# A gated slot attention block with a linear layer: the first tiles of the last phase begin a step sooner, between the products of the last step

## The chip, the core and the metric

The kernel runs on one core of one Trainium2 chip. The metric is the device time of one launch in microseconds (us); lower is better. Nothing else runs on the chip.

## The reference

Four sequences of 512 rows with 512 columns go through an attention block with 16 heads of width 128 and 64 memory slots per head, then a residual sum and layer norm, then a linear layer (called FFN here) with its own residual sum and layer norm. What follows is the core of it (float32):

```python
q, k = rope(hs @ Wq.T), rope(hs @ Wk.T)              # 16 heads of 128
v, g = hs @ Wv.T, hs @ Wg.T
s = clip(hs @ Ws1.T @ Ws2.T + bs2, -32, 32)          # 64 slots per head
es, enz = exp(s), exp(-cumlogsumexp(s, axis=time))
A  = mask(q k^T) * scale
ok = enz * (A @ es);  qv = softmax(ok)
W2 = mask((qv * enz) @ es^T);  o = W2 @ v
o_g = o * rsqrt(mean(o*o) + EPS) * g_norm_weight * (g * sigmoid(g))
x = layernorm(hs + o_g @ Wo.T)
out = layernorm(x + x @ (weight * scale_weight[:, None]).T + bias)
```

## The kernel before, in words

**Steps.** The 2048 rows are 16 chunks of 128, the 16 heads are 4 groups of 4. One step does one chunk for one group, so there are 64 steps (STEPS), four chunks of a sequence in a row (c = 0 to 3), unrolled by `all_steps_in_line`. `left` is the number of chunks still to come in the sequence where this is the last sequence of the last group: it is 1 in step 63 and 0 in step 64; in most steps it is 4. A step projects the next chunk (q, k, v, gate) and does the attention of this one. Matrix products in float32 are split into a high and a low part (names `_hi`, `_lo`): three products of 128x512 for each of four column blocks, which makes 12 instructions (`product`, line 874). The gated and normalised output `o_gated` of a step is transposed into `oT`, split into `oT_hi` (ScalarE) and `oT_lo` (VectorE), multiplied by Wo in the next step and added by VectorE to a partial sum `part`, which SyncE stores to a scratch in DRAM and loads again for the next group.

**Last phase.** 16 tiles of 128 rows go through norm, linear layer and norm. A function `tick(t, s)` on each engine does tick t: VectorE takes the statistics of tile t (`first_stats`, `first_mean_var`, `first_neg_mean`, `first_var_eps`), adds the linear layer's product of tile t-4 to its residual, takes that one's statistics, and between them makes the low part of the transposed rows of tile t-2. GpSimd makes x1 + bias of tile t-2 and two powers (1/sqrt of var + eps) for tile t and tile t-4. ScalarE makes the high part of the transposed rows of tile t-1, the normalised rows x1 of tile t, and the output rows z of tile t-4, and issues the store of these. TensorE makes the linear layer's 12 products of tile t-2 and 4 transposes of x1 of tile t. Ticks 0 to 3 stand inside step 64 (`if not left`) and behind it, tick 4 to 7 are written out (`last_phase`), then a loop runs.

**Order.** Every engine executes its own instructions in the order in which they are written, and waits on semaphores that the others raise. So where a `tick` is written in `step` sets what it waits behind and what waits behind it. In step 64 before: TensorE does the okT products (line 983, 988), the transposes of step 63's o_gated (L888), tick 0 (transposes of x1 row tile 0, L961), okT's transposes, prob's transposes (L888, 128x128 x2), step 63's Wo product (bank_a), the w2 and states products (L1051, L1055), tick 1, tick 2 (product of tile 0 and transposes of tile 2), the o products (L1076); then, behind the step, tick 3, the last transposes of o_gated, the last Wo product (`last_out`) and tick 4. VectorE does tick 0 before `ok_scaled`, tick 1 before `part`, tick 2 before `mask_w2`, tick 3 after it. GpSimd does `o_norm` of the step before first (a power L429 and a product L431, which normalise o_gated), then the ticks. ScalarE does tick 0 first, ticks 1 and 2 before `o_sq`, tick 3 behind the step, then `oT_hi`.

**Names in the trace.** A buffer that is used again keeps its first name: the raw rows of the last phase and x1 are `w_raw`, the transposed rows' parts are `w_hi` and `w_lo` (`bank_c`, `bank_e`, `bank_a`, `bank_wo` are their banks), the linear layer's products are written into `bank_qv`, `bank_kg`, `bank_t` and `bank_wo`, and z into `gate`, `masked` and `rope_a`. `x1 + bias` goes to `q_rot`, `k_rot`, `qT`. The two banks `bank_s` and `bank_o` are the halves of `bank_wo`.

## Time and profile before

| | us |
|---|---|
| median of three runs | 1488.28 (1487.54, 1488.28, 1490.73) |
| the profiled execution | 1487.25 |
| its span in the trace | 1485.4 |
| TensorE busy (page, part 1) | 1455.7 (98% of the span) |
| VectorE, ScalarE, GpSimd busy | 912.0, 526.9, 506.5 |
| mean granted TensorE clock | 0.998 |

The profile has one page with the busy time of each engine and, behind it, a trace of each instruction. In the timeline a line is the start (us from the span's start), the duration, the engine (PE is TensorE, DVE VectorE, ACT ScalarE, POOL GpSimd, SPq and ACTq DMA issues by SyncE and ScalarE), the line of the kernel, what is written and read, how many instructions are merged, and in brackets the idle time before it with the engine that ended it. The duration of a matmul includes its way through the array, so that two in a row overlap; the distance between two starts is what one costs. Steps 63 and 64 end at about 1409 and 1427 us; the last store is issued at the end of the span.

### The profile page before, as it was taken

The numbers are of one execution on the slowest core, as the hardware profiler recorded it, in microseconds if no ns is written. First come the engines' busy times: TensorE is split into PE (matmuls) and PEld (weight loads), VectorE is DVE, ScalarE is ACT, GpSimd is POOL, SyncE is SP. The second block draws the span as 40 slices with busy tenths as digits, with TensorE's granted clock in tenths as the row PEclk, the third lists the DMA queues.
The fourth block names the chain that finished last, engine by engine and source line by source line (L and its number), as shares of the span: only waits on it lengthen the run. The fifth ranks groups of instructions, "written<-read, shape, count | busy, mean of one in ns | idle before, by whom it ended". The sixth has DMA issues, their size and how long they took to land.

```text
span 1485.4 us, 22855 instructions
## 1 busy us (share of the span) xinstructions
PE 1455.7 (98%) x9152; PEld 1193.2 (80%) x9152; DVE 912.0 (61%) x1651; ACT 526.9 (35%) x1013; POOL 506.5 (34%) x440
## 2 busy tenths in 40 slices
PE   6999999999999999999999999999999999999988
PEld 4888888888888888888888888888888888888866
DVE  6656556566665656556765655656765565656677
ACT  5323323234322323333332333323433332324256
POOL 2333233233242233224423322422432242333245
PEclk9999999999999999999999999999999999999999
DMA  5101102122111202112320211112221111202123
GB/s 205 65 22 62 53 22 72 38 84 99 65 58 43 72 22 72 43 36 79 135 72 22 72 43 36 58 43 93 86 99 44 36 58 43 71 22 78 65 89 124
DMA packets 39558, 96.60 MB, mean 65 GB/s; under 512 B 4384, under 2 KB 4384, under 8 KB 35744
## 3 DMA queue, kind: packets, MB, share of 16 engines
q1 hardware_dynamic: 37152, 90.98, 18.3%
q10 hardware_dynamic: 2304, 4.20, 0.8%
q8 instruction: 72, 1.18, 0.3%
q14 instruction: 30, 0.25, 0.1%
HBM read 74.19 MB, written 20.97 MB: 64 GB/s over the span
## 4 chain that ended last, share of the span: by engine, by line
PE 89%; POOL 5%; DVE 2%; issue 2%; ACT 1%; DMA 0%; SPq 0%; POOLq 0%; DVEq 0%; ACTq 0%
PE bank_kg L874 25%; PE bank_qv L874 22%; PE bank_a L874 12%; PE bank_t L888 7%; PE bank_wo L1076 4%; POOL o_gated L431 3%; PE bank_a L909 3%; PE bank_e L901 3%; PE bank_wo L1051 3%; PE bank_wo L983 2%; PE bank_c L1081 2%; PE bank_wo L1055 1%; POOL rms L429 1%; PE bank_c L1086 1%; PE bank_wo L916 1%
## 5 line engine op out<-in xcount | busy, mean ns | idle before, releaser
L429 POOL TENSOR_TENSOR rms<-var,minus_half 128x4 f32<-128x4 f32 x64 | 65.2, 1018 | 594.2 <-DVE var L846 594.2
L874 PE MATMUL bank_qv<-w_hi,hs_hi 128*128 128x512 f32 x512 | 209.6, 409 | 7.2 <-DVE w_lo L627 6.8
L874 PE MATMUL bank_kg<-w_hi,hs_hi 128*128 128x512 f32 x512 | 207.6, 406 | 3.3 <-DVE w_lo L627 3.3
L874 PE MATMUL bank_qv<-w_hi,hs_lo 128*128 128x512 f32 x512 | 204.1, 399 | 0.0
L874 PE MATMUL bank_qv<-w_lo,hs_hi 128*128 128x512 f32 x512 | 203.4, 397 | 0.0
L874 PE MATMUL bank_kg<-w_hi,hs_lo 128*128 128x512 f32 x512 | 202.7, 396 | 0.0
L874 PE MATMUL bank_kg<-w_lo,hs_hi 128*128 128x512 f32 x512 | 201.9, 394 | 0.0
L874 PE MATMUL bank_a<-wo_hi,oT 128*128 128x512 f32 x504 | 171.8, 402 | 0.0
L400 POOL TENSOR_TENSOR k_rot<-rope_a,rope_b 128x512 f32<-128x512 f32 x64 | 82.6, 1290 | 223.6 <-DVE rope_b L656 223.6
L697 DVE RECIPROCAL enzT<-cumsT 128x256 f32<-128x256 f32 x64 | 112.2, 1753 | 63.9 <-ACT cumsT L514 51.7
L465 ACT ACTIVATE oT<-bank_t 128x512 fp32r<-128x512 f32 x64 | 38.3, 598 | 262.6 <-PE bank_t L888 262.6
L396 POOL TENSOR_TENSOR q_rot<-rope_a,rope_b 128x512 f32<-128x512 f32 x64 | 82.6, 1290 | 115.0 <-DVE rope_b L656 115.0
L874 PEld LDWEIGHTS bank_qv<-w_hi,hs_hi 128*128 128x128 f32 x512 | 97.5, 190 | 26.1 <-issue 7.5
L874 PEld LDWEIGHTS bank_qv<-w_hi,hs_lo 128*128 128x128 f32 x512 | 96.9, 189 | 23.4
L874 PEld LDWEIGHTS bank_kg<-w_hi,hs_lo 128*128 128x128 f32 x512 | 96.1, 188 | 23.1
L874 PEld LDWEIGHTS bank_kg<-w_hi,hs_hi 128*128 128x128 f32 x512 | 96.3, 188 | 21.3 <-DVE w_lo L627 2.5
L874 PEld LDWEIGHTS bank_qv<-w_lo,hs_hi 128*128 128x128 f32 x512 | 97.3, 190 | 17.4
L874 PEld LDWEIGHTS bank_kg<-w_lo,hs_hi 128*128 128x128 f32 x512 | 96.4, 188 | 17.6
L874 PEld LDWEIGHTS bank_a<-wo_hi,oT 128*128 128x128 f32 x504 | 94.8, 188 | 18.1
L798 DVE TENSOR_REDUCE ok_max<-bank_wo 128x4 f32<-128x256 f32 x64 | 27.2, 424 | 132.4 <-PE bank_wo L1015 132.4
L431 POOL TENSOR_TENSOR o_gated<-o_gated,rms 128x512 f32<-128x512 f32 x64 | 98.2, 1534 | 5.0
L827 DVE TENSOR_TENSOR part<-bank_a,part 128x512 f32<-128x512 f32 x63 | 43.4, 690 | 91.6 <-PE bank_a L874 91.6
(163 smaller groups left out, 2921.3 us busy)
## 6 DMA issues: line engine op xcount, KB each, us to landing
w_raw<-w_groups SPq DMA_DIRECT2D x28, 1024.0 KB, 4.8
hs_raw<-hs_cols SPq DMA_DIRECT2D x64, 256.0 KB, 2.8
x_scratch<-part SPq DMA_DIRECT2D x64, 256.0 KB, 2.0
part<-x_scratch SPq DMA_DIRECT2D x48, 256.0 KB, 2.7
w_raw<-w_groups SPq DMA_DIRECT2D x16, 256.0 KB, 6.1
part<-hs_rows SPq DMA_DIRECT2D x16, 256.0 KB, 2.7
w_raw<-x_scratch SPq DMA_DIRECT2D x16, 256.0 KB, 2.7
out<-gate ACTq DMA_DIRECT2D x8, 256.0 KB, 2.2
```

The lines of the kernel that those rows point to most:

```text
L396: pool.tensor_tensor(q_rot[:, :], rope_a[:, :], rope_b[:, :], ALU.add).then_inc(q_summed, 1)
L400: pool.tensor_tensor(k_rot[slot][:, :], rope_a[:, :], rope_b[:, :], ALU.add).then_inc(k_summed, 1)
L429: pool.tensor_tensor(rms[:, :], var[:, :], minus_half[:, :], ALU.pow).then_inc(rms_made, 1)
L431: pool.tensor_tensor(per_head(o_gated[:, :]), per_head(o_gated[:, :]), over_columns(rms[:, :], DV), ALU.mult).then_inc(o_norm_made, 1)
L697: dve.reciprocal(enzT[:, :], cumsT[slot][:, :])
L827: dve.tensor_tensor(part[c % 2][:, :], bank_a[:, :], part[c % 2][:, :], ALU.add).then_inc(part_made, 1)
L874: mm = pe.matmul(dst, x, y, start=start and n == 0, stop=stop and n == 2, **kw)
L888: mm = pe.transpose(bank_t[:, P * h:P * h + P], src[:, P * h:P * h + P], ident)
L901: mm = pe.matmul(bank_e[:, 2 * P * r:2 * P * r + 2 * P], half[slot][:, P * r:P * r + P], ident_keep[:, :], start=x == 0, stop=x == 1)
L909: mm = pe.matmul(bank_a[:, P * h:P * h + P], kT[:, P * h:P * h + P], qT[:, P * h:P * h + P], start=True, stop=True)
L1051: mm = pe.matmul(w2_of(h), esT[rows, at], pT[rows, at], start=True, stop=True)
L1076: mm = pe.matmul(o_of(h), masked[:, head], v[now][:, head], start=False, stop=True, skip_group_check=True)
```

## The change

Ticks 0 and 1 of VectorE and GpSimd, and tick 0 of ScalarE, move from step 64 to the end of step 63. Within step 64 ScalarE does tick 1 first, tick 2 behind oT_hi and ahead of prob's exponential, tick 3 ahead of `o_sq`; VectorE does tick 2 behind oT_lo and ahead of `ok_max`, tick 3 ahead of `part`; GpSimd has ticks 2 and 3 left. TensorE's tick is taken apart into `ffn` (products) and `turn_x1` (transposes): transposes of tile 0 ahead of the okT products, of tile 1 ahead of okT's transposes, product 0 ahead of prob's transposes, transposes of tile 2 ahead of the o products, product 1 behind them, then transposes of tile 3, the last transposes of o_gated (into bank_o), product 2, the last Wo product (into bank_a), transposes of tile 4. ScalarE and VectorE do tick 4 ahead of the last oT_hi and oT_lo; VectorE adds the last part behind tick 5. SyncE loads the first four x rows in step 63. The diff, without blank lines:

```diff
             return ap.unsqueeze(2).broadcast_to([P, ap.shape[1], n])
-        def last_phase(eng, lag_max, tick, before=LAST, after={}):
-            for t in range(LAST, before):
+        def last_phase(eng, lag_max, tick, begin=LAST, before=LAST, after={}):
+            for t in range(begin, before):
                 tick(t, t % LAST)
                 if t in after:
                     after[t]()
...
                     sp.dma_start(w_raw[1][:, :], ffn_w).then_inc(w_in[1], 16)
                     sp.dma_start(scale_row[:, :], ffn_scale.partition_broadcast(P)).then_inc(scale_in, 16)
-                if not left:
+                if left == 1:
                     sp.wait_ge(wf_hi_made, 1)
                     sp.wait_ge(wf_lo_made, 1)
                     for j in range(LAST):
                         load_row(j, j)
+                if not left:
                     sp.wait_ge(k_summed, STEPS)
                     sp.dma_start(bias_row[:, :], ffn_bias.partition_broadcast(P)).then_inc(bias_in, 16)
                 chunk = c - 2 if last and c >= 2 else b * CB + (c + 2)
...
                     o_norm(done(u, c) - 1)
                 if left:
                     q_sum(done(u, c, 1))
-                else:
-                    tick(0, 0)
                 if left >= 2:
                     hs_split(c % 2, done(u, c, 2))
                 if left:
...
                         pool.wait_ge(w_hi_made, g * 4 + 2)
                         pool.tensor_tensor(w_lo[WK][:, :], w_raw[SLOT[WK]][:, :], w_hi[WK][:, :].bitcast(F32),
                                            ALU.subtract).then_inc(wk_lo_made, 1)
+                    if left == 1:
+                        tick(0, 0)
+                        tick(1, 1)
                 else:
-                    tick(1, 1)
                     pool.wait_ge(bias_in, 16)
                     tick(2, 2)
                     tick(3, 3)
...
                 if left >= 2:
                     hs_split(c % 2, (u * (CB // 2) + (c // 2 + 2)) * 16)
                 if not left:
-                    tick(0, 0)
+                    tick(1, 1)
                 if i > 1:
                     from_bank(oT_hi, bank_t[:, :], oT_mm, i - 1, oT_hi_made)
+                if not left:
+                    tick(2, 2)
                 if n <= CHUNKS:
                     u_hi(n)
                 if last and c == 2:
...
                     act.activation(gate[(c + 1) % 2][:, :], bank_kg[:, :], ACT.Tanh, scale=0.5).then_inc(th_made, 1)
                     from_bank(kT[:, :], bank_t[:, :], kT_mm, n, kT_made)
                 if not left:
-                    tick(1, 1)
-                    tick(2, 2)
+                    tick(3, 3)
                 act.wait_ge(o_mm, i)
                 act.activation(by_parity(o_sq[:, :]), paired(1), ACT.Square).then_inc(o_squared, 1)
                 if c < CB - 1:
                     from_bank(states[:, :], bank_c[:, :], states_mm, carried(u, c), states_made)
+                if left == 1:
+                    tick(0, 0)
             all_steps_in_line(step)
-            tick(3, 3)
-            from_bank(oT_hi, bank_t[:, :], oT_mm, STEPS, oT_hi_made)
-            last_phase(act, 4, tick, before=2 * LAST)
+            tick(4, 0)
+            from_bank(oT_hi, bank_o[:, :], oT_mm, STEPS, oT_hi_made)
+            last_phase(act, 4, tick, begin=5, before=2 * LAST)
         @block.vector
         def _(dve):
...
                     w_split_half(WV, g * 4 + 3, 0)
                 if left:
                     rotate_q((c + 1) % CB, n)
-                else:
-                    tick(0, 0)
                 dve.wait_ge(okT_mm, i)
                 dve.scalar_tensor_tensor(okT, okT_acc, SCALE, enzT[:, :], ALU.mult, ALU.mult).then_inc(ok_scaled, 1)
                 if i > 1:
                     lo(oT_lo, bank_t[:, :], oT_hi, oT_hi_made, i - 1, oT_lo_made)
+                if not left:
+                    tick(2, 2)
                 if n <= CHUNKS:
                     u_lo(n)
                 if last and c == 3:
...
                 if left == CB - 2:
                     split_ffn()
                 if not left:
-                    tick(1, 1)
+                    tick(3, 3)
                 if i > 1:
                     dve.wait_ge(out_mm, i - 1)
                     dve.wait_ge(part_in[c % 2], parts_of(c % 2, u * (CB // 2) + c // 2 + 1) * 16)
                     dve.tensor_tensor(part[c % 2][:, :], bank_a[:, :], part[c % 2][:, :], ALU.add
                                       ).then_inc(part_made, 1)
-                if not left:
-                    tick(2, 2)
                 mask_w2(i)
-                if not left:
-                    tick(3, 3)
                 if left:
                     make_enz((c + 1) % 2, n)
                     make_gate((c + 1) % 2, n)
...
                                          ).then_inc(var_made, 1)
                 if left:
                     mask_a(n)
+                if left == 1:
+                    tick(0, 0)
+                    tick(1, 1)
                 if c == 0:
                     dve.wait_ge(wo_hi_made, u + 1)
                     dve.scalar_tensor_tensor(wo_lo[:, :], w_raw[0][:, :], gn, wo_hi[:, :].bitcast(F32),
...
             all_steps_in_line(step)
             def last_oT():
-                lo(oT_lo, bank_t[:, :], oT_hi, oT_hi_made, STEPS, oT_lo_made)
+                lo(oT_lo, bank_o[:, :], oT_hi, oT_hi_made, STEPS, oT_lo_made)
             def last_part():
                 dve.wait_ge(out_mm, STEPS)
                 dve.wait_ge(part_in[0], STEPS // 2 * 16)
-                dve.tensor_tensor(part[0][:, :], bank_o[:, :], part[0][:, :], ALU.add).then_inc(part_made, 1)
+                dve.tensor_tensor(part[0][:, :], bank_a[:, :], part[0][:, :], ALU.add).then_inc(part_made, 1)
+            tick(4, 0)
             last_oT()
-            last_phase(dve, 4, tick, before=2 * LAST, after={LAST: last_part})
+            tick(5, 1)
+            last_part()
+            last_phase(dve, 4, tick, begin=6, before=2 * LAST)
         @block.tensor
         def _(pe):
...
             transposes(k_rot[0]).then_inc(kT_mm, 1)
             scores(1)
+            def ffn(j, slot):
+                pe.wait_ge(x1T_lo_made, j + 1)
+                for k in range(KT):
+                    mm = product(banks_ffn[slot][:, :], cols((x1T_hi[slot], x1T_lo[slot]), P * k, P),
+                                 cols((wf_hi, wf_lo), D * k, D), start=k == 0, stop=k == KT - 1)
+                mm.then_inc(ffn_mm, 1)
+            def turn_x1(j, slot):
+                pe.wait_ge(norm_sems[FIRST][ROWS], j + 1)
+                for k in range(KT):
+                    mm = pe.transpose(banks_T[slot][:, P * k:P * k + P], x1[slot][:, P * k:P * k + P], ident)
+                mm.then_inc(x1T_mm, 1)
             def tick(t, s):
                 j, slot, there = staged(t, s, 2)
                 if there:
-                    pe.wait_ge(x1T_lo_made, j + 1)
-                    for k in range(KT):
-                        mm = product(banks_ffn[slot][:, :], cols((x1T_hi[slot], x1T_lo[slot]), P * k, P),
-                                     cols((wf_hi, wf_lo), D * k, D), start=k == 0, stop=k == KT - 1)
-                    mm.then_inc(ffn_mm, 1)
+                    ffn(j, slot)
                 j, slot, there = staged(t, s, 0)
                 if there:
-                    pe.wait_ge(norm_sems[FIRST][ROWS], j + 1)
-                    for k in range(KT):
-                        mm = pe.transpose(banks_T[slot][:, P * k:P * k + P], x1[slot][:, P * k:P * k + P], ident)
-                    mm.then_inc(x1T_mm, 1)
+                    turn_x1(j, slot)
             def step(u, g, b, c, last, left):
                 i, n = done(u, c), done(u, c, 1)
...
                         w_ready(g * 4 + 1, g * 3 + 1)
                     project(WQ, bank_qv, nxt).then_inc(q_mm, 1)
+                if not left:
+                    pe.wait_ge(states_made, carried(u, c - 1))
+                    turn_x1(0, 0)
                 pe.wait_ge(a_masked, i)
                 if c:
                     pe.wait_ge(states_made, carried(u, c - 1))
...
                 if n <= CHUNKS:
                     low_rank(nxt)
                 if not left:
-                    pe.wait_ge(wf_lo_made, 1)
-                    tick(0, 0)
+                    pe.wait_ge(cumsT_made, 2 * i)
+                    turn_x1(1, 1)
                 if left:
                     pe.wait_ge(gate_made, i)
...
                 for r in range(2):
                     mm = pe.transpose(ok_acc[:, P * r:P * r + P], okT[:, P * r:P * r + P], ident)
                 mm.then_inc(ok_mm, 1)
+                if not left:
+                    pe.wait_ge(wf_lo_made, 1)
+                    ffn(0, 0)
                 if left:
                     if last and c == CB - 1:
                         pe.wait_ge(ws2_made, 6)
...
                     pe.wait_ge(k_summed, n)
                     transposes(k_rot[nxt]).then_inc(kT_mm, 1)
                 if not left:
-                    tick(1, 1)
                     pe.wait_ge(part_made, i - 1)
-                    tick(2, 2)
+                    turn_x1(2, 2)
                 pe.wait_ge(w2_masked, i)
                 for h in range(HG):
...
                 return ws2_part[:, bass.ds(g * H, H)]
             all_steps_in_line(step)
+            ffn(1, 1)
             pe.wait_ge(o_gated_made, STEPS)
-            tick(3, 3)
+            turn_x1(3, 3)
             pe.wait_ge(o_norm_made, STEPS)
-            transposes(o_gated).then_inc(oT_mm, 1)
+            for h in range(HG):
+                mm = pe.transpose(bank_o[:, P * h:P * h + P], o_gated[:, P * h:P * h + P], ident)
+            mm.then_inc(oT_mm, 1)
+            ffn(2, 2)
             def last_out():
                 pe.wait_ge(oT_lo_made, STEPS)
                 for h in range(HG):
-                    mm = product(bank_o[:, :], cols((oT_hi, oT_lo), P * h, P), cols((wo_hi, wo_lo), D * h, D),
+                    mm = product(bank_a[:, :], cols((oT_hi, oT_lo), P * h, P), cols((wo_hi, wo_lo), D * h, D),
                                  start=h == 0, stop=h == HG - 1)
                 mm.then_inc(out_mm, 1)
             last_out()
-            last_phase(pe, 2, tick)
+            turn_x1(4, 0)
+            last_phase(pe, 2, tick, begin=5, before=2 * LAST, after={5: lambda: pe.wait_ge(part_made, STEPS)})
 def kernel(**inputs):
```

## Rows read from the trace of the kernel before

**Rows 1.** Windows: stretch, length; busy time of each engine; granted clock, DMA share, GB/s
```profile
1409.00:1438.30 29.30, 22.22 (x133) 17.59 (x134) 18.68 (x54) 11.14 (x21) 12.05 (x14) 1.00 0.18 56
1438.30:1480.00 41.70, 40.82 (x200) 33.26 (x198) 37.89 (x121) 31.96 (x62) 28.48 (x37) 1.00 0.40 138
```

**Rows 2.** Timeline, TensorE: start, duration (us), instruction [idle before, releaser]
```profile
1409.71 0.66 PE L983 MATMUL bank_wo<-masked,es 128*64 128x128 f32 x8 [0.78 <-DVE masked L701]
...
1412.66 0.63 PE L961 MATMUL bank_c<-small_ops,w_raw 128*128 128x128 f32 x4 [1.12 <-ACT w_raw L548]
...
1415.02 0.44 PE L888 MATMUL bank_t<-small_ops,prob 128*128 128x128 f32 x2 [1.51 <-ACT prob L591]
...
1420.41 0.47 PE L874 MATMUL bank_qv<-wf_hi,w_hi 128*128 128x512 f32 x1 [0.52 <-DVE w_lo L627]
...
1423.24 0.60 PE L961 MATMUL bank_a<-small_ops,w_raw 128*128 128x128 f32 x4
1423.68 1.06 PE L1076 MATMUL bank_wo<-v,masked 128*128 128x128 f32 x8
1426.15 0.49 PE L874 MATMUL bank_kg<-wf_hi,w_hi 128*128 128x512 f32 x1 [1.41 <-DVE o_gated L841]
...
1431.46 0.50 PE L874 MATMUL bank_wo<-wo_hi,oT 128*128 128x512 f32 x1 [1.41 <-DVE oT L627]
...
1441.19 0.47 PE L874 MATMUL bank_qv<-wf_hi,w_hi 128*128 128x512 f32 x1
```

**Rows 3.** Timeline, VectorE
```profile
1409.57 0.69 DVE L738 BATCH_NORM_STATS2 first_stats<-w_raw 128x6 f32<-128x512 f32 x1
...
1410.58 0.14 DVE L749 TENSOR_SCALAR first_var_eps<-first_mean_var 128x1 f32<-128x1 f32 x1
...
1418.25 0.69 DVE L827 TENSOR_TENSOR part<-bank_a,part 128x512 f32<-128x512 f32 x1 [1.19 <-PE bank_a L874]
...
1438.30 0.68 DVE L738 BATCH_NORM_STATS2 first_stats<-w_raw 128x6 f32<-128x512 f32 x1
...
1440.39 0.69 DVE L627 TENSOR_TENSOR w_lo<-bank_c,w_hi 128x512 fp32r<-128x512 f32 x1
...
1441.45 0.68 DVE L738 BATCH_NORM_STATS2 first_stats<-w_raw 128x6 f32<-128x512 f32 x1
```

**Rows 4.** Timeline, GpSimd
```profile
1408.70 1.02 POOL L429 TENSOR_TENSOR rms<-var,minus_half 128x4 f32<-128x4 f32 x1 [9.82 <-DVE var L846]
...
1410.80 0.55 POOL L423 TENSOR_TENSOR first_rstd<-first_var_eps,minus_half 128x1 f32<-128x1 f32 x1
...
1427.03 1.02 POOL L429 TENSOR_TENSOR rms<-var,minus_half 128x4 f32<-128x4 f32 x1 [3.53 <-DVE var L846]
...
1429.12 1.27 POOL L417 TENSOR_TENSOR k_rot<-w_raw,rope_b 128x512 f32<-128x512 f32 x1
```

**Rows 5.** Timeline, ScalarE
```profile
1411.71 0.81 ACT L548 ACTIVATE w_raw<-w_raw,first_shift,first_rstd 128x512 f32<-128x512 f32 x1
...
1436.48 0.82 ACT L548 ACTIVATE gate<-kT,second_shift,second_rstd 128x512 f32<-128x512 f32 x1
1437.33 0.38 ACTq L565 DMA_DIRECT2D out<-gate  x1
```

**Rows 6.** Timeline, SyncE's loads; then the page's DMA issues (to landing in us)
```profile
1437.61 6.12 SPq L317 DMA_DIRECT2D w_raw<-x_scratch  x3
...
w_raw<-x_scratch SPq DMA_DIRECT2D x16, 256.0 KB, 2.7
```

**Rows 7.** Timeline, TensorE at the start of the kernel
```profile
14.04 0.50 PE L874 MATMUL bank_kg<-w_hi,hs_hi 128*128 128x512 f32 x1 [1.81 <-DVE w_lo L627]
...
19.04 0.63 PE L888 MATMUL bank_t<-small_ops,q_rot 128*128 128x128 f32 x4 [1.94 <-POOL q_rot L396]
...
19.98 0.63 PE L874 MATMUL bank_qv<-w_hi,hs_lo 128*128 128x512 f32 x1
...
22.97 0.58 PE L874 MATMUL bank_qv<-w_hi,hs_hi 128*128 128x512 f32 x1
```

## The prediction

> **What bounds the kernel now.** I read the stretches of the last step and of the final phase first, then TensorE's order of work between them, then the three engines that feed it. The change touches nothing before the end of the last but one step. From 1438.3 us on TensorE is busy 40.82 of 41.70 us, and VectorE is nearly full too, 37.89 [rows 1]. In the 29.3 us before, TensorE is busy 22.22: about 7.1 us of holes, all there is to win. In TensorE's own order [rows 2] they stand as bracketed idle times: 0.78 us (masked scores), 1.12 (row 0 of x1), 1.51 (prob), 0.52 (x1T_lo of tile 0), 1.41 (o_gated of step 64) and 1.41 (last oT). A hole counts from the drained end of the matmul before; by starts each is some 0.2 us longer.
>
> The steady phase is tight on two engines. VectorE's tick takes 3.15 us, start of stats to start of stats, and its x1T_lo begins 2.09 us in [rows 3]; TensorE's tick (12 products, 2.83 from 1420.41 to 1423.24, and 4 transposes, 0.44 from there to 1423.68 [rows 2]; a little less in the steady phase) takes 3.2. So a delay of VectorE's tick 6 comes out at the end one for one, and the same holds for tile 4's product. I carry the new order up to these two.
>
> **The change part by part.** All instructions stay; only order and two banks change. I count from the last scores of step 63, which drain at 1408.93 (the next matmul starts at 1409.71 after 0.78 idle [rows 2]).
>
> *Ticks 0 and 1 move to the end of step 63.* On VectorE they stand behind mask_a(64), which needs those scores, so tick 0's stats still start at 1409.57 and its var_eps still ends at 1410.72 [rows 3]. Tick 0 begins no sooner there; tick 1 follows at once and gives its var_eps at 1411.80 (1.15 us for a tick without x1T_lo). On GpSimd the two powers now stand ahead of o_norm(63). That was ready to start at 1408.70, and with it first tick 0's power came at 1410.80 [rows 4]. Now power 0 takes 1410.80 to 1411.35, power 1 waits for 1411.80 and ends at 1412.43, and only then o_norm(63), 2.1 us, ends at 1414.5 instead of 1410.8: **3.7 us later**. Row 0 comes from ScalarE at 1412.52 as before [rows 5].
>
> *Row 0's transposes stand ahead of the last step's scores products.* They wait for ScalarE and start at 1412.66, as before [rows 2], but now the okT products queue behind them: 1413.10 instead of 1409.71. The hole is 3.74 us. okT ends about 1414.1; the transposes of o_gated wait for GpSimd until 1414.6; row 1's transposes go at 1415.05 and okT's at 1415.5 to 1415.7.
>
> *Tick 2 moves ahead of ok_max on VectorE and ahead of prob's exponential on ScalarE.* ScalarE's oT_hi ends at 1415.8; VectorE's oT_lo at 1416.6; tick 2's stats start 1416.5, x1T_lo(0) is there at 1417.9, var_eps at 1418.2. TensorE, idle since 1415.7, starts product 0 at 1418.0 and ends it at 1420.86. ScalarE must wait for GpSimd's power (1418.85), make row 2 (to 1420.0), and gives prob at 1420.4. That is under product 0, so prob's hole of 1.51 is covered; had product 0 not been there it would show in full. Prob's transposes start at 1420.86 instead of 1415.02: 5.84 later with 3.27 us more work done (row 1's transposes 0.44, product 0 2.83). **Loss so far 2.6 us.**
>
> *Middle of the step.* From prob's transposes to the end of the w2 and states products was 4.2 us: product 0 started at 1420.41 after 0.52 idle, row 1's transposes before it took 0.66 to drain, so they started at 1419.23, 4.21 after 1415.02 [rows 2]. Now these end at 1425.07. VectorE adds the part 3.23 us after prob's transposes [rows 3], at 1424.1; tick 3 ahead of it fits into its wait. Row 2's transposes end at 1425.5, mask_w2 (0.69) at 1425.86, the o products start at 1425.93 (1423.68 before) and product 1 at 1426.82, without the 1.41 us hole. It stood at 1426.15: **still 0.67 us late**, so this part wins 1.9.
>
> *The last oT and out.* From the o products' start to the power of o_norm(64) took 3.35 us [rows 2, 4]; row 3 on ScalarE adds 0.2, so it starts at 1429.5 and o_gated is ready at 1431.6. Product 1 and row 3's transposes end at 1430.1: a hole of 1.56. Transposes to 1432.1, product 2 to 1434.98. But ScalarE now makes oT_hi behind its whole tick 4: GpSimd has o_norm to 1431.55, the bias sum (1.27 [rows 4]), power of row 4 to 1433.35, power of y row 0 to 1433.87. ScalarE makes row 4, then z row 0 (start to transfer 0.85 us, issue 0.38 [rows 5]), and oT_hi ends near 1436.6, oT_lo at 1437.3. The last out waits for it **2.4 us**, 1437.36 to 1440.23. VectorE, idle from 1432.5 to 1436.6, runs tick 5, then the last part at 1440.44, and tick 6 from 1441.04 instead of 1438.30. Tile 4's product starts at 1443.95 (VectorE 2.8 us into tick 6) instead of 1441.19.
>
> The queues' price is therefore 2.6 - 1.9 + 2.1 = **2.8 us**.
>
> *The transfers.* The first four x rows now go out near 1380, the others behind part_made(63). Rows 8 on follow the last store, which is 5.9 us later; before, they were issued at 1437.61 [rows 6], now about 1443.5, and are needed at 1447.3 (tick 8). A landing time of 2.7 us [rows 6] leaves 1 us. I cost them at nothing; without that margin each microsecond counts. Other banks: nothing, no reader is late.
>
> *TensorE's clock.* At the start of the kernel, behind holes of 1.81 and 1.94 us, some products ran at 1.2 GHz instead of 2.4: seven of them take 2.99 us by starts (0.43 each against 0.23), a loss of 1.4 us [rows 7]; that is the lower of the two levels. Between 1409 and 1438 it stays 1.00 with holes up to 1.51 [rows 1, 2]. The new order has two places worse than that: 3.74, 0.45 and 2.3 us with 1.9 and 0.9 us of work between, and 1.56 and 2.4 us with 3.3 us between. No row shows such a pair here, so the price lies between nothing and one fall for each of the three large holes, 4.2 us. I take two falls at 1.4, since the first place is far beyond the start's. In the first, doubling 1.9 us of work also costs 1.4 after the hole of 0.45 takes its share.
>
> The Trainium skill (TensorE: Matmul & The Clock Gate, section "HAM oscillation") says that idle gaps between bursts of matmuls bring the array back to half rate, paid again at every burst; the start of this trace agrees, the end does not show it yet.
>
> **Sum.** Profiled execution 1487.25 (span 1485.4 and 1.85 around it) + 2.8 + 2.8 = **1492.8 us**. The three runs have 1487.54, 1488.28 and 1490.73; the profiled one lies 1.0 under their median, which the range takes in.
>
> **Rivals.**
> 1. *Queues alone, no fall of the clock*: 1487.25 + 2.8 = 1490.0. For it: 1.00 with six holes now. Against it: the 3.74 us hole is twice the start's. Chance 0.17.
> 2. *One fall*: 1491.4, chance 0.20; *three falls*: 1494.2, chance 0.15.
> 3. *The last oT isn't late* (ScalarE's tick 4 ends before 1434.3, for instance because z row 0 costs less): the 2.4 us hole goes and with it a fall: 1487.25 + 0.4 + 1.4 = 1489.0; without any fall 1487.6. Against it: GpSimd's bias and two powers stand in between. Chance 0.08.
> 4. *Faster*: the products fill the holes as placed. If the x1 rows are ready by 1408.9, o_norm(63) isn't held, prob (1.51), x1T_lo (0.52), o_gated (1.41) and oT (1.41) lie under work, and 4.85 us go: 1482.4. It decides where tick 0's stats start; they would have to start 3.7 us sooner than 1409.57. The order behind mask_a speaks against it. Chance 0.06.
>
> The forecast, two falls, has 0.34.
>
> **How the numbers follow.** 0.2% is 3 us, about what a measurement of this kernel can tell from no change; the border is 1491.3. Slower: two and three falls 0.49, most of one fall (0.17 of 0.20, as the median lies above the profiled run) and 0.08 of rival 1's 0.17, for the same offset: 0.74. Faster: rival 4, 0.06. Same: the rest, 0.20. Range: 1489.4 (rival 1 less 0.6) to 1495.5 (three falls and the offset of 1.0), leaving out rival 4, most of rival 3 and the top, under 2 in 10.
>
> **What would show it.** After the change: a TensorE hole of about 3.7 us before row 0's transposes at 1412.7; o_norm's power starting near 1412.4; the power for x1's row 2 before prob's exponential; a hole of some 2.4 us before the last out with oT_hi behind the transfer of z row 0; the granted clock under 1.00 in slices after 1412. I am wrong if okT starts at 1409.7, if VectorE's tick 6 starts before 1438.3, or if the products after the holes stand 0.23 us apart throughout.

## The result, and the profile after

The changed kernel takes 1494.25 us (median of 7 runs, 1492.33 to 1496.24) against 1488.28 (7 runs, 1487.54 to 1490.73): the ratio is 1.0035 with an interval of 1.0023 to 1.0046, so it is slower by 0.35%. Its profiled execution has 1495.56 us (span 1493.7), the one before 1487.25 (span 1485.4).

The two profiled executions differ by 8.31 us. The last scores of step 63 start at 1408.48 us instead of 1407.76, so 0.72 us of it arose before, in a part that the change doesn't touch; the first scores of the kernel are already 0.76 us apart (30.67 and 31.43). The product of tile 4 starts at 1449.49 instead of 1441.19 [rows 2]. Between these two points before took 33.43 us and after takes 41.01, 7.58 more; from there to the end of the span both take 44.21 us. I call this stretch, from the start of the last scores to the start of tile 4's product, **the join**. It leaves out what the start of the kernel does, though not a fall of the clock inside it, and is the measure for the experiments. The medians differ by less than the two profiled executions, 5.97 us.

TensorE's timeline of the changed kernel over the join (columns as in [rows 2], line 880 is the products' line, 965 the transposes of x1, 1093 the o products):

```profile
1408.48 1.16 PE L915 MATMUL bank_a<-qT,kT 128*128 128x128 f32 x8
1413.39 0.63 PE L965 MATMUL bank_c<-small_ops,w_raw 128*128 128x128 f32 x4 [3.75 <-ACT w_raw L549]
...
1415.30 1.12 PE L894 MATMUL bank_t<-small_ops,o_gated 128*128 128x128 f32 x4
...
1419.24 0.77 PE L880 MATMUL bank_qv<-wf_hi,w_hi 128*128 128x512 f32 x1 [1.55 <-DVE w_lo L631]
1419.80 0.63 PE L880 MATMUL bank_qv<-wf_lo,w_hi 128*128 128x512 f32 x1
...
1424.50 0.63 PE L894 MATMUL bank_t<-small_ops,prob 128*128 128x128 f32 x2
...
1430.69 0.48 PE L880 MATMUL bank_kg<-wf_hi,w_hi 128*128 128x512 f32 x1
...
1435.57 0.66 PE L1121 MATMUL bank_wo<-small_ops,o_gated 128*128 128x128 f32 x4 [1.43 <-POOL o_gated L432]
...
1441.31 0.50 PE L880 MATMUL bank_a<-wo_hi,oT 128*128 128x512 f32 x1 [2.31 <-DVE oT L631]
...
1445.76 0.60 PE L965 MATMUL bank_c<-small_ops,w_raw 128*128 128x128 f32 x4
...
1449.49 0.47 PE L880 MATMUL bank_qv<-wf_hi,w_hi 128*128 128x512 f32 x1
```

Tile 0's transposes wait 3.75 us for row 0. From there the okT products and the transposes of o_gated (1415.30) queue up. Product 0 starts at 1419.24, and its second product 0.56 us behind its first: prob's transposes come 5.26 us after product 0's start, where 12 products took 2.83 before [rows 2]. The hole of 1.41 us ahead of product 1 is gone (1430.69, no idle time), but the last out waits 2.31 us (1441.31) and then takes 4.45 us to the next transposes (1445.76) instead of the 2.9 that it took before.

GpSimd's queue, against [rows 4]:

```profile
1411.51 0.56 POOL L424 TENSOR_TENSOR first_rstd<-first_var_eps,minus_half 128x1 f32<-128x1 f32 x1 [11.92 <-DVE first_var_eps L753]
1412.58 0.56 POOL L424 TENSOR_TENSOR first_rstd<-first_var_eps,minus_half 128x1 f32<-128x1 f32 x1 [0.51 <-DVE first_var_eps L753]
1413.11 1.02 POOL L430 TENSOR_TENSOR rms<-var,minus_half 128x4 f32<-128x4 f32 x1
1414.20 1.04 POOL L432 TENSOR_TENSOR o_gated<-o_gated,rms 128x512 f32<-128x512 f32 x1
```

Two powers run from 1411.51 on, and the power of o_norm(63) starts only at 1413.11, although VectorE had made its operand `var` by 1409.27, as early as before. ScalarE's row 0, its tick 4 (z row 0, the transfer's issue, then oT_hi), and VectorE's last oT_lo and the start of tick 6:

```profile
1412.43 0.81 ACT L549 ACTIVATE w_raw<-w_raw,first_shift,first_rstd 128x512 f32<-128x512 f32 x1
...
1438.66 0.81 ACT L549 ACTIVATE gate<-kT,second_shift,second_rstd 128x512 f32<-128x512 f32 x1
1439.50 0.39 ACTq L566 DMA_DIRECT2D out<-gate  x1
1439.94 0.60 ACT L466 ACTIVATE oT<-bank_wo 128x512 fp32r<-128x512 f32 x1 [0.47 <-ACT gate L549]
...
1440.57 0.69 DVE L631 TENSOR_TENSOR oT<-bank_wo,oT 128x512 fp32r<-128x512 f32 x1 [4.17 <-ACT oT L466]
...
1446.57 0.68 DVE L742 BATCH_NORM_STATS2 first_stats<-w_raw 128x6 f32<-128x512 f32 x1
```

oT_hi stands right behind the issue of z row 0, as in the order of the code, and VectorE has waited 4.17 us for it. The clock, in windows (start and end, length, busy time of TensorE's matmuls and weight loads, VectorE, ScalarE and GpSimd, granted clock, DMA):

```profile
1409.00:1414.00 5.00, 1.25 (x12) 0.92 (x11) 2.92 (x11) 1.30 (x3) 1.98 (x3) 1.00 0.00 0
1414.00:1420.00 6.00, 4.34 (x29) 3.49 (x29) 3.24 (x9) 2.79 (x5) 2.89 (x4) 0.56 0.01 3
1420.00:1426.00 6.00, 6.00 (x19) 4.70 (x18) 1.47 (x5) 1.41 (x3) 1.30 (x2) 0.58 0.00 0
...
1440.00:1447.00 7.00, 5.69 (x20) 4.57 (x21) 4.77 (x13) 1.14 (x3) 2.33 (x3) 0.76 0.10 39
```

Between 1414 and 1426 us the mean granted clock is 0.56 and 0.58, from 1440 to 1447 it is 0.76; before it was 1.00 throughout [rows 1].

### The profile page after: what moved, and what is told of

Same layout as the page of the kernel before. It is cut to its first block, busy times and chain, and to the rows that moved or that the text cites. A ratio compares the mean times of both kernels' runs of the same rounds, so it can differ in the third digit from the quotient of the medians.

```text
span 1493.7 us, 22851 instructions
## 1 busy us (share of the span) xinstructions
PE 1462.5 (98%) x9152; PEld 1197.6 (80%) x9152; DVE 912.7 (61%) x1651; ACT 527.0 (35%) x1013; POOL 507.0 (34%) x440
## 4 chain that ended last, share of the span: by engine, by line
PE 89%; POOL 5%; DVE 3%; issue 2%; ACT 1%; DMA 0%; POOLq 0%; ACTq 0%; SPq 0%
PE bank_kg L880 24%; PE bank_qv L880 22%; PE bank_a L880 12%; PE bank_t L894 7%; PE bank_wo L1093 4%; PE bank_a L915 3%; POOL o_gated L432 3%; PE bank_e L907 3%; PE bank_wo L1069 3%; PE bank_wo L998 2%; PE bank_c L1098 2%; PE bank_wo L1073 1%; POOL rms L430 1%; PE bank_c L1103 1%; PE bank_wo L922 1%
## 5 line engine op out<-in xcount | busy, mean ns | idle before, releaser
L880 PE MATMUL bank_a<-wo_hi,oT 128*128 128x512 f32 x512 | 175.8, 404 | 2.3 <-DVE oT L631 2.3
L880 PE MATMUL bank_a<-wo_lo,oT 128*128 128x512 f32 x256 | 100.8, 394 | 0.0
```

Of the source, the lines that this page charges most:

```text
L880: mm = pe.matmul(dst, x, y, start=start and n == 0, stop=stop and n == 2, **kw)
```

## The experiments

The times of the join, from the profiled execution of each kernel, beside the medians. "Before" is the median of the kernel before, measured together with the kernel of its row; it moves by up to 1.2 us between the rows, so medians of different groups are best compared by their distance from it.

| kernel | join, us | median, us | before, us | ratio and interval |
|---|---|---|---|---|
| before | 33.43 | | | |
| changed | 41.01 | 1494.25 | 1488.28 | 1.0035 (1.0023 to 1.0046) |
| r1 oT_hi first | 36.31 | 1490.43 | 1488.72 | 1.0009 (0.9999 to 1.0020) |
| r2 row 0 behind okT | 40.80 | 1496.39 | 1488.72 | 1.0051 (1.0036 to 1.0066) |
| r3 o_norm first | 36.92 | 1494.56 | 1488.72 | 1.0036 (1.0023 to 1.0048) |
| r4 kept busy | 36.30 | 1491.57 | 1488.72 | 1.0017 (1.0008 to 1.0026) |
| r5 end alone | 35.42 | 1488.42 | 1487.91 | 0.9998 (0.9988 to 1.0007) |
| r6 end, oT_hi first | 31.20 | 1485.97 | 1487.91 | 0.9982 (0.9973 to 0.9991) |
| r7 early loads | 33.50 | 1487.90 | 1487.91 | 0.9996 (0.9987 to 1.0005) |
| r8 rows in step 63 | 27.58 | 1482.48 | 1487.91 | 0.9953 (0.9939 to 0.9967) |
| r9 two queues open | 40.16 | 1492.66 | 1489.13 | 1.0027 (1.0017 to 1.0037) |
| r10 three queues open | 33.88 | 1489.53 | 1489.13 | 1.0002 (0.9987 to 1.0016) |

**r4: clock and queues apart.** Products that nobody reads fill three holes. The order of the queues stays; one wait is added (`gate_made`, for the bank that the products write), so the "no wait" of the expectation is not quite so.

```diff
+            def idle_products(n):
+                for _ in range(n):
+                    pe.matmul(bank_kg[:, :], hs_hi[0][:, 0:P], w_hi[WQ][:, 0:F], start=True, stop=True)
...
+                    pe.wait_ge(gate_made, STEPS)
+                    idle_products(14)
                     pe.wait_ge(states_made, carried(u, c - 1))
                     turn_x1(0, 0)
...
+                    idle_products(8)
                     pe.wait_ge(wf_lo_made, 1)
                     ffn(0, 0)
...
             def last_out():
+                for _ in range(9):
+                    pe.matmul(banks_T[0][:, :], hs_hi[0][:, 0:P], w_hi[WQ][:, 0:F], start=True, stop=True)
```

> The changed kernel with products that nobody reads in three holes of TensorE: 14 ahead of tile 0's transposes, 8 ahead of product 0, 9 ahead of the last out (0.23 us each, 3.3, 1.9 and 2.1 us, a little less than the holes). No wait and no queue changes. My account: the holes cost 2.8 us by order and bring the clock down besides; with the holes filled the granted clock stays 1.00 from 1400 us on, the queues' 2.8 us stay, and the time is 4 to 5 us below 1494.25, near 1490. Rival: the clock falls for another reason, or its fall costs nothing on this path; then the time stays at 1494 or goes up by what the products overrun.

TensorE's timeline and two windows of it:

```profile
1411.18 1.16 PE L915 MATMUL bank_a<-qT,kT 128*128 128x128 f32 x8
1412.10 3.51 PE L964 MATMUL bank_kg<-w_hi,hs_hi 128*128 128x512 f32 x14
1416.10 0.63 PE L969 MATMUL bank_c<-small_ops,w_raw 128*128 128x128 f32 x4 [0.49 <-ACT w_raw L549]
...
1421.49 0.47 PE L880 MATMUL bank_qv<-wf_hi,w_hi 128*128 128x512 f32 x1 [0.24 <-DVE w_lo L631]
...
1424.32 0.38 PE L894 MATMUL bank_t<-small_ops,prob 128*128 128x128 f32 x2
...
1438.43 2.26 PE L1134 MATMUL bank_c<-w_hi,hs_hi 128*128 128x512 f32 x9
1440.88 0.50 PE L880 MATMUL bank_a<-wo_hi,oT 128*128 128x512 f32 x1 [0.19 <-DVE oT L631]
...
1447.48 0.47 PE L880 MATMUL bank_qv<-wf_hi,w_hi 128*128 128x512 f32 x1
```

```profile
1414.00:1420.00 6.00, 5.26 (x41) 3.99 (x41) 2.23 (x9) 3.81 (x7) 4.38 (x5) 1.00 0.00 0
1420.00:1426.00 6.00, 5.76 (x27) 4.41 (x26) 4.02 (x13) 1.42 (x3) 1.81 (x2) 1.00 0.00 0
```

In the three places the idle times shrink to 0.49 and less, and the clock stays 1.00 up to 1480 us; a hole of 1.43 us before the last transposes of o_gated is left as it was. Product 0 takes 2.83 us again (1421.49 to 1424.32). The join is 36.30 us: with the clock up, the order costs 2.87 us more than before, and the 4.71 us up to 41.01 in the changed kernel's profiled execution are the clock's. In medians it is 2.85 us above its before, where the changed kernel is 5.97 above its own: 3.1 us are the clock's in a typical run, uncertain by some 2 us by the two intervals. Adding 31 useless products makes the kernel faster; an account by queues alone would have made it no faster.

**r1: the last oT.** The changed kernel with ScalarE's two lines swapped:

```diff
-            tick(4, 0)
             from_bank(oT_hi, bank_o[:, :], oT_mm, STEPS, oT_hi_made)
+            tick(4, 0)
```

> The changed kernel with one line moved: ScalarE makes the last oT_hi ahead of its tick 4. My account: oT_hi no longer stands behind the row of tile 4 and z of tile 0, so the last out starts right behind product 2, the hole of 2.3 us goes and with it the second stretch at the lower clock (1.6 us): about 4 us below the changed kernel's 1494.25, near 1490.3. Rival: what is late is VectorE's tick 4 or the bank, then the hole stays within 0.4 us and the time within 0.5 us of 1494.25.

TensorE around the last out, then ScalarE's oT_hi:

```profile
1439.79 0.39 PE L880 MATMUL bank_t<-wf_hi,w_lo 128*128 128x512 f32 x1
1440.02 0.39 PE L880 MATMUL bank_a<-wo_hi,oT 128*128 128x512 f32 x1
...
1437.43 0.60 ACT L466 ACTIVATE oT<-bank_wo 128x512 fp32r<-128x512 f32 x1 [4.55 <-PE bank_wo L1121]
```

The last out (1440.02) follows product 2 without a gap, and oT_hi runs at 1437.43, as soon as its transposes are there. The median is 1490.43, 3.8 us below the changed kernel's, as expected (1490.3); by the distances from their own befores it is 4.3, by the joins 4.7. The second stretch at the lower clock went with the hole: from 1440 to 1447 us the clock is 1.00. The bank and VectorE's tick 4 are not what was late.

**r2 and r3: one of the first half's queues at a time.** r2 puts tile 0's transposes behind okT; r3 puts o_norm(63) ahead of both powers.

```diff
-                if not left:
-                    pe.wait_ge(states_made, carried(u, c - 1))
-                    turn_x1(0, 0)
...
                 mm.then_inc(okT_mm, 1)
 
+                if not left:
+                    turn_x1(0, 0)
```

> The changed kernel with TensorE's transposes of x1 tile 0 behind the okT products instead of ahead of them. My account: two queues hold the same place. okT starts 3.4 us sooner (about 0.8 us behind the scores), but o_gated's transposes still wait for GpSimd's o_norm, which stands behind two powers; product 0 and prob keep their times within 0.3 us, and only the clock may fall at another place: 1492.5 to 1494.5. Rival: the transposes ahead of okT are the loss by themselves; then 3.4 us go and the time is near 1490.9.

```diff
-                    if left == 1:
-                        tick(0, 0)
-                        tick(1, 1)
                 else:
+                    tick(0, 0)
+                    tick(1, 1)
                     pool.wait_ge(bias_in, 16)
```

> The changed kernel with GpSimd's o_norm(63) ahead of the powers of ticks 0 and 1. My account: okT is still held by tile 0's transposes, so o_gated's transposes gain only the 0.45 us that they waited behind okT: 1493.8, the clock falling as before. Rival: o_norm's 3.7 us are the loss by themselves; then the time is near 1490.5.

TensorE's timeline of r2 (line 995 okT, 965 tile 0, 894 o_gated):

```profile
1410.92 0.66 PE L995 MATMUL bank_wo<-masked,es 128*64 128x128 f32 x8 [0.78 <-DVE masked L705]
...
1413.80 0.66 PE L965 MATMUL bank_c<-small_ops,w_raw 128*128 128x128 f32 x4 [1.78 <-ACT w_raw L549]
1415.79 1.11 PE L894 MATMUL bank_t<-small_ops,o_gated 128*128 128x128 f32 x4 [1.34 <-POOL o_gated L432]
...
1419.74 0.76 PE L880 MATMUL bank_qv<-wf_hi,w_hi 128*128 128x512 f32 x1 [1.55 <-DVE w_lo L631]
```

okT starts 0.78 us behind the drained scores, 3.5 us sooner (1.94 us behind their start against 5.47). But o_gated's transposes (1415.79) and product 0 (1419.74) come 6.81 and 10.76 us after the last scores' start (1408.98), in the changed kernel 6.82 and 10.76: nothing gained. One hole of 3.75 us has become two of 1.78 and 1.34, and the median rises to 1496.39 (four runs), 1.9 us above the upper end of what I expected. Its join, 40.80, is that of the changed kernel; whether the rest is more than the clock's chance in four runs stays open. In r3 product 0 starts 10.91 us behind the last scores' start, nothing gained either, and the median is 1494.56 where I expected 1493.8. Its profiled execution is the fastest of its six runs (1490.77) and has a join of 36.92, 4.1 us less than the changed kernel's. Nearly all of that is the clock: it was back at 1.00 before product 0 started, so that from product 0 to prob's transposes it took 2.84 us against 5.26, and it did not fall again at the last out, 2.86 against 4.45.

**r9 and r10: two and three queues.** r9 has r3's edit and tile 0's transposes behind those of o_gated. r10 has ScalarE's oT_hi of step 63 ahead of tick 1 besides:

```diff
-                if not left:
-                    tick(1, 1)
                 if i > 1:
                     from_bank(oT_hi, bank_t[:, :], oT_mm, i - 1, oT_hi_made)
                 if not left:
+                    tick(1, 1)
                     tick(2, 2)
```

> The changed kernel with two of its three queues opened: GpSimd's o_norm(63) ahead of the powers, and TensorE's transposes of tile 0 behind those of o_gated. My account: okT and o_gated's transposes then come as in the kernel before, but ScalarE makes x1T_hi(0) and row 1 ahead of oT_hi and so keeps it 2.4 us late; product 0 and prob come no sooner than with o_norm alone moved (product 0 about 10.9 us behind the last scores' start), only the holes are smaller and the clock falls less: from the last scores to product 4 35.5 to 37 us. Rival: the two opened queues were the loss; then product 0 comes 2 us sooner and 34 us.

> The same with the third opened too: ScalarE's oT_hi of step 63 ahead of its tick 1. My account: oT_hi ends 5.2 us behind the last scores' start as in the kernel before (9.0 in the changed kernel's order of r9), product 0 starts near 6.7 and prob's transposes near 9.9 us behind it, so the first half loses nothing; what is left is the late last oT: 33.0 to 34 us from the last scores to product 4, and 1488 to 1489.5 us. Rival: no more than 0.5 us below r9; then the loss lies in something that I haven't named.

ScalarE in r9, row 1 and then oT_hi, and TensorE's product 0:

```profile
1415.82 0.81 ACT L548 ACTIVATE w_raw<-w_raw,first_shift,first_rstd 128x512 f32<-128x512 f32 x1
1416.53 0.58 ACT L465 ACTIVATE oT<-bank_t 128x512 fp32r<-128x512 f32 x1
...
1419.31 0.76 PE L879 MATMUL bank_qv<-wf_hi,w_hi 128*128 128x512 f32 x1 [1.69 <-DVE w_lo L630]
```

and in r10 oT_hi, and TensorE's product 0:

```profile
1414.82 0.58 ACT L465 ACTIVATE oT<-bank_t 128x512 fp32r<-128x512 f32 x1
...
1418.03 0.47 PE L878 MATMUL bank_qv<-wf_hi,w_hi 128*128 128x512 f32 x1
```

Behind the last scores' start oT_hi starts at 7.02 us in r9 (1409.51) and at 4.67 in r10 (1410.15), product 0 at 9.80 and 7.88. So r9 gained 1.0 us on product 0, which I had not expected, but missed the join: I had 35.5 to 37 and the clock fell all the same, 40.16. r10's 33.88 lies in what I expected, though not by its parts: product 0 comes 1.2 us later than I had, since row 1 of x1 keeps tile 1's transposes waiting. With three queues opened the first half costs nothing any more; what is left is the last out, which still waits 2.27 us for oT. Of the smaller sets, one queue each (r2, r3) and this pair (r9) didn't do it; oT_hi's queue alone and the other pairs were not run.

**r5 and r6: the second half alone**, on the kernel before; r6 with r1's swap. Not shown: the last out into bank_a, and ScalarE's and VectorE's tick 4 ahead of the last oT_hi and oT_lo.

```diff
             all_steps_in_line(step)
+            ffn(1, 1)
             pe.wait_ge(o_gated_made, STEPS)
-            tick(3, 3)
+            turn_x1(3, 3)
             pe.wait_ge(o_norm_made, STEPS)
-            transposes(o_gated).then_inc(oT_mm, 1)
+            for h in range(HG):
+                mm = pe.transpose(bank_o[:, P * h:P * h + P], o_gated[:, P * h:P * h + P], ident)
+            mm.then_inc(oT_mm, 1)
+            ffn(2, 2)
```

> The kernel before with the second half of the change alone: step 64 up to the o products as before, behind them product 1, transposes of tile 3, last transposes into bank_o, product 2, last out into bank_a, ScalarE's and VectorE's tick 4 ahead of the last oT_hi and oT_lo. My account: product 1 gains the 1.41 us hole, but oT_hi stands behind ScalarE's tick 4, so the last out comes at about the time that it needs tick 4's z row, a hole of 2.4 us; the sum from the last scores to product 4 is 33.8 us against 33.4, 1489 to 1490 us. Rival: the whole loss comes from this half; then 1494.

> The same with the last oT_hi ahead of ScalarE's tick 4. My account: product 1 lies under o_gated's wait and product 2 under oT's, so 2.0 us go: from the last scores to product 4 31.4 us against 33.4, 1486.7 against 1488.7 of the kernel before, no hole before the last out. Rival: VectorE's tick 4 ahead of its last oT_lo takes the gain back; then no difference from the kernel before.

r5 (1488.42, no difference from before) still has the hole ahead of the last out. TensorE's prob transposes, one product of the out of step 63, tile 1's transposes, and the last out:

```profile
1419.38 0.64 PE L891 MATMUL bank_t<-small_ops,prob 128*128 128x128 f32 x2 [1.51 <-ACT prob L591]
...
1420.24 0.63 PE L877 MATMUL bank_a<-wo_lo,oT 128*128 128x512 f32 x1
...
1425.17 0.66 PE L962 MATMUL bank_e<-small_ops,w_raw 128*128 128x128 f32 x4
...
1440.90 0.50 PE L877 MATMUL bank_a<-wo_hi,oT 128*128 128x512 f32 x1 [2.31 <-DVE oT L627]
```

and the last out of r6:

```profile
1433.01 0.39 PE L877 MATMUL bank_a<-wo_hi,oT 128*128 128x512 f32 x1
```

r5's last out waits 2.31 us. The product of step 63's out lasts 0.63 us, the length at the lower clock: in this execution the clock fell (0.76 from 1420 to 1426 us) behind holes of 0.78, 1.12 and 1.51 us, the very holes of the kernel before, which in [rows 2] did nothing. From prob's transposes to tile 1's it takes 5.79 us against 4.21 before; that explains a join of 35.42 against the 33.8 expected. With oT_hi first (r6) the hole goes (no idle time at 1433.01) and the kernel is 1.9 us faster than before, a ratio of 0.9982 with an interval below 1; the join, 31.20, was to be 31.4.

**r7: the loads alone.**

```diff
-                if not left:
+                if left == 1:
                     sp.wait_ge(wf_hi_made, 1)
                     sp.wait_ge(wf_lo_made, 1)
                     for j in range(LAST):
                         load_row(j, j)
+                if not left:
```

> The kernel before with nothing but the loads of the first four x rows in step 63 instead of 64. My account: no difference, within 0.5 us, because the rows are there in both before VectorE reads them. Rival: the moved transfers hold up SyncE's queue; then part of the loss shows here, 1 us or more.

1487.90 against 1487.91, join 33.50: the moved loads cost nothing.

**r8: the rows ready before the scores end.** The changed kernel with r1's swap and, in VectorE's part and then ScalarE's, ticks 0 and 1 in the middle of step 63. Not shown: VectorE's tick 2 goes from behind oT_lo, ScalarE's tick 0 from the end of step 63, and its tick 1 becomes x1T_hi(0) alone.

```diff
+                if left == 1:
+                    tick(0, 0)
+                    tick(1, 1)
                 if not left:
                     tick(3, 3)
 
                 if i > 1:
                     dve.wait_ge(out_mm, i - 1)
...
                     mask_a(n)
                 if left == 1:
-                    tick(0, 0)
-                    tick(1, 1)
+                    tick(2, 2)
...
+                if left == 1:
+                    rows(FIRST, 0, 0, x_row[0], x1[0])
+                    rows(FIRST, 1, 1, x_row[1], x1[1])
                 if left:
                     turned((c + 1) % 2, n, c == CB - 1)
```

> The changed kernel with what I named as the point from which it would be faster: VectorE's ticks 0 and 1 ahead of the part of step 63, in its wait there, ScalarE's rows 0 and 1 ahead of the turned sums of step 63, VectorE's tick 2 behind mask_a, ScalarE's x1T_hi(0) first in step 64, and oT_hi ahead of tick 4. Rows 0 and 1 and their powers are then ready before the last scores end. My account: tile 0's transposes start at once, okT as before, product 0 lies under prob's wait, products 1 and 2 under o_gated's and oT's; from the last scores to product 4 27.4 us against 33.4, 1482.5 to 1483. Rival: step 63 gets longer by the work put into it (VectorE's 2.2 us in a wait of 1.7), or the order on TensorE is a loss by itself; then 1486 or more.

TensorE, then GpSimd's first power and ScalarE's row 0:

```profile
1411.19 1.16 PE L917 MATMUL bank_a<-qT,kT 128*128 128x128 f32 x8
1412.19 0.60 PE L967 MATMUL bank_c<-small_ops,w_raw 128*128 128x128 f32 x4
1413.13 0.66 PE L1000 MATMUL bank_wo<-masked,es 128*64 128x128 f32 x8 [0.35 <-DVE masked L707]
...
1415.39 0.48 PE L882 MATMUL bank_qv<-wf_hi,w_hi 128*128 128x512 f32 x1
...
1418.23 0.38 PE L896 MATMUL bank_t<-small_ops,prob 128*128 128x128 f32 x2
...
1438.77 0.47 PE L882 MATMUL bank_qv<-wf_hi,w_hi 128*128 128x512 f32 x1
```

```profile
1403.49 0.56 POOL L424 TENSOR_TENSOR first_rstd<-first_var_eps,minus_half 128x1 f32<-128x1 f32 x1 [1.17 <-DVE first_var_eps L755]
...
1404.41 0.81 ACT L549 ACTIVATE w_raw<-w_raw,first_shift,first_rstd 128x512 f32<-128x512 f32 x1
```

The first power runs at 1403.49 and row 0 at 1404.41, ahead of the last scores (1411.19). Tile 0's transposes follow these at once, okT waits 0.35 us, and product 0 and prob's transposes have no idle time before them. The join is 27.58 (27.4 expected) and the median 1482.48: 5.4 us faster than before, ratio 0.9953 (0.9939 to 0.9967). It beats both kernels. How much of it is due to the earlier rows alone wasn't run: r1's swap, in it too, is worth 2.2 us of join in r6.

## Why the prediction was right, point by point

**The queues.** Times behind the last scores' start, at the 2.4 GHz level in the prediction and in r4:

| | predicted | r4 | changed |
|---|---|---|---|
| tile 0's transposes | 4.90 | 4.92 | 4.91 |
| product 0 | 10.27 | 10.31 | 10.76 |
| prob's transposes | 13.10 | 13.14 | 16.02 |
| product 1 | 19.06 | 19.09 | 22.21 |
| last out | 29.60 | 29.70 | 32.83 |
| product of tile 4 | 36.19 | 36.30 | 41.01 |

The reading in order of each engine's queue held within 0.11 us at each point, and the price of 2.8 us is 2.87 measured in r4. Each step named was seen: o_norm behind two powers (GpSimd), okT behind tile 0's transposes, prob behind row 2 (ScalarE makes row 2 and then prob, and prob's transposes start in r4 when product 0 ends), oT_hi behind z row 0.

**The loads** cost nothing (r7), the later last store neither: from product 4 to the end of the span the changed kernel takes 44.21 us as before, and VectorE waited for no transfer in it, so no tick waited for its x row.

**The clock.** The forecast took two falls at 1.4 us. The profiled execution has two stretches at the lower level, but the term was mis-sized there: 4.71 us instead of 2.8. The price of one fall was the weak step: it was taken from the start of the kernel, where seven products ran slow. In the changed kernel all twelve of product 0 ran slow, and before them the transposes of o_gated and tile 1 (the first lasts 1.12 us, in r4 0.66): prob's transposes come 2.88 us later than in r4, and the last out 3.13 us, more than twice the 1.4. The second fall cost 1.58 us (4.45 us for the last out against 2.87), near the 1.4. In the median the clock's part is 3.1 us, near the 2.8 forecast, but that agreement is in part luck: no trace shows a run near the median, and whether two falls took place in it isn't shown.

The Trainium skill (TensorE: Matmul & The Clock Gate, section "HAM oscillation") says that waits between bursts of matmuls bring the array back to the lower rate and that the next burst pays for it; r4 agrees, where the same order with three gaps filled keeps 1.00 and is 3.1 us faster than the changed kernel, each against its own before.

**The sum.** 1492.8 was forecast, 1494.25 measured. The sum stood on a profiled execution 1.0 us below its median; with that offset it would have been 1493.9. The upper end of the range, 1495.5, is 0.3 us above what its own terms give (1494.2 and 1.0 are 1495.2); nothing hangs on it.

**The rivals.** Queues without a fall of the clock: r4 is that case, and it needed the products. The last oT not late: not so, 2.31 us. The faster case was said to hinge on where tick 0's stats start, 3.7 us sooner than they do; in r8 they start 8.93 us ahead of the last scores' start instead of 1.81 behind it, and the kernel gains 5.4 us, where I had 4.85 for the four holes. But that rival counted the hole before the last out (1.41 us) as filled by the same step, which it isn't: in r10, whose first half loses nothing, the last out still waits 2.27 us, and r8 has the swap of oT_hi besides.

## What to carry to other kernels

When a step is moved into another step, write down for each engine what now stands behind it and when its operand is there; here three engines held back the same chain: opening GpSimd's or TensorE's queue alone brought nothing at product 0, both together 1.0 us, and all three 2.9 us. Fill a hole only with work whose inputs are ready before the hole begins, or the filler becomes what everyone waits for. One line, oT_hi ahead of a tick that it doesn't need, was worth 3.8 us of the median in the changed kernel and 2.5 us between r5 and r6.

## What the runs showed of the hardware that I had not expected

TensorE's clock falls at other places from execution to execution. Behind holes of 0.78, 1.12 and 1.51 us it stayed at 1.00 in the kernel before and fell in r5. TensorE's order of work up to the last scores is the same in all these kernels, and yet they start between 1407.76 us (before) and 1412.12 (r5), and the mean granted clock of the first 30 us goes from 0.87 (r4) to 1.00 (r6). The clock is not all of that spread: r6, with 1.00, reaches the last scores at 1408.27, later than the kernel before with 0.94; what else moves them stays open. So the time of a single execution can't price a change of 3 us. The distance between two instructions around the change leaves out the start, and a variant with the holes filled leaves out the falls between them.

The Trainium skill (TensorE: Matmul & The Clock Gate, section "What's actually happening") says that the number of slow matmuls varies from run to run of the same kernel; the granted clocks just named, 0.87 to 1.00 over the same first work, agree.
